# A fused conv/attention kernel: prologue in its own order, and q and k projected by three rounded products

## The chip, the cores and the metric

The kernel runs on one core of one Trainium2 chip. The metric is the device time of one execution in microseconds (us), as the median of the runs shown. Names of engines: PE is TensorE (matmul; PEld is its weight load), DVE is VectorE, ACT is ScalarE, POOL is GpSimd, SP is the sync engine that issues the DMAs.

## The reference, cut to what matters

The input is x of 16 images, 128 channels, 16 by 16 pixels, all float32. Four blocks follow each other.

```
L0: q = x as (b, 128, 256); energy = q q^T; attention = softmax(max - energy)
    out = attention q; se = sigmoid(w2 relu(w1 mean([x, out]))); x1 = se*x + (1-se)*out
L1: xr = relu(bn(depthwise3x3(reduce_w x1)))            # 64 channels
    2-D Fourier transform, 8-head attention on it, inverse transform; a gated filter
    x2 = post_w [out, filtered] + post_b + x1
L2: xn = group_norm(x2); q, k, v = w_qkv xn; 8-head attention over 256 pixels
    x3 = w_proj h + b_proj + x2
L3: q3, k3, v3 = conv3x3(x3); attention over the 16 images per pixel; layernorm; relu; conv3x3; + x3
```

## The kernel before, in words

**Tiling.** Images are handled in 8 pairs; channels lie on the 128 partitions and the two images of a pair side by side (512 columns). Each engine has one program written out by hand, and semaphores join them.

**Stages.** Blocks L0, L1 and the group norm are cut into small stages (function `stage(what, i)`, once per engine, for pair i): `energy`, `e_min`, `att0`, `att0t`, `o0`, `hid0`, `z0`, `se`, `x1` are L0; `red`, `taps0` to `taps2`, `xr`, `hid1`, `z1`, `xh`, `xht`, `dft`, `ab`, `squares`, `dot1`, `logit1`, `att1`, `even`, `filt`, `patt`, `post_att`, `y1`, `x2` are L1; `gsum`, `gvar`, `grstd`, `xn` are the group norm. `gvar` (L961) has four small DVE steps; `xn` (L970) has three small steps and two of 128x256.

**Slots.** `slots(j, late, early, cj)` is the body of a pair, 24 slots per engine: L2's attention of pair j, the L1 stages of pair j+1 (`late`), the L0 stages of pair j+2 (`early`) and the convolutions of L3 on the finished pair j-1 (`cj`). The tables `PE_SLOTS`, `ACT_SLOTS`, `DVE_SLOTS`, `POOL_SLOTS` (L65 to L71) say in which slot each stage stands. At the end of a body PE projects q and k of pair j+1 (`project`, L1345), ACT and DVE split them into a rounded and a low part (`qk_high_parts`, `qk_low_parts`), and the next body's scores need those. The convolutions and other products that must be exact are made of three products of operands rounded to fp32r (high*high, high*low, low*high). The projection uses one plain float32 product of 128x512 for each of its four blocks (L1358); the hardware runs each as two instructions.

**The prologue.** Before the first body, each engine walks its table for L0 of pair 0, then for L0 of pair 1 with L1 of pair 0 (L1084 to L1089 on DVE, L1587 to L1600 on PE). Before that DVE and PE wait for the first constants (`cst_loaded`, L857, L1575): DVE prepares seven small values, PE multiplies one bias. SP issues the loads in the order x_t (x by pixels, for the energies), x_in, first constants, second constants, weights. All stages of L1 take their matmul results from PSUM bank 1, each waiting until the stage before has read it. The program keeps PE occupied with idle products (`keep_busy`, L1249, matmuls of `ones_r`) in counts given by the `BUSY_` constants. For pairs 0 and 1 four of the nine depthwise taps are PE matmuls (`taps`, L1577); for the rest all nine are DVE operations (L900, L903).

## Time and profile before

| | |
|---|---|
| median of 3 runs | 492.95 us (491.77 to 495.27) |
| the profiled execution | 491.87 us, of which its span is 490.1 us |
| prologue, to the first score product of pair 0 | 44.1 us |
| bodies of pairs 0 and 1 | 44.1 to 134 us |
| bodies of pairs 2 to 6 | 134 to 359 us, 45.0 us each |
| body of pair 7, L3's attention, last convolutions | 359 to 490 us |

A row of the timeline gives the start, the length, the engine, the source line, the operation, what it writes from what, the shapes and a count; in brackets stands how long the engine had been idle and what ended that. A row of the chain of waits gives the start, the length and what ran: it is followed back from the last instruction, so that each piece was what the next one waited for. A row of stages gives for each stretch the busy time of each engine with the number of instructions, then TensorE's granted clock as a share of full speed and the DMA's load.

### The profile page before, as it was taken

Reading aid. Unit: us, or ns where it says so; the run is one execution under the profiler, and the core shown is the slowest. Engines: PE = TensorE matmul, PEld = TensorE weight load, DVE = VectorE, ACT = ScalarE, POOL = GpSimd, SP = SyncE. Lnnn points to the kernel's source line nnn. Section 1 sums busy time; section 2 is a strip of 40 time slices with the busy share of each in tenths; the row PEclk is TensorE's granted clock in tenths of the full one; section 3 lists DMA queues with packets and bytes.
Section 4 is the critical chain, followed back from the end, with each engine's and each line's share of the span. In section 5 each row is a group of like instructions: output and inputs, shape, how many; then the busy total and the mean of one; then the engine's idle time right before and its main releaser. Section 6 shows DMA issues by size and latency. Waiting matters only on the chain.

```text
span 490.1 us, 10552 instructions
## 1 busy us (share of the span) xinstructions
PE 462.6 (94%) x3790; PEld 371.5 (76%) x3790; DVE 342.4 (70%) x890; ACT 248.6 (51%) x590; POOL 125.3 (26%) x154
## 2 busy tenths in 40 slices
PE   8999999898999999999999999999997999998896
PEld 7876865676587778777776877777775789898895
DVE  1438567977787778688777877787476443776895
ACT  3434656665555555645656555545534531394551
POOL 5121363375012103101211121020110011332672
PEclk9999999999899999999999999999997999998998
DMA  7100012030002001000100000000000000005112
GB/s 274 36 32 3 1 49 91 1 93 24 0 1 60 7 0 43 21 0 0 43 21 0 0 21 0 2 22 3 0 1 23 1 23 1 1 1 171 45 56 73
DMA packets 10639, 15.28 MB, mean 31 GB/s; under 512 B 624, under 2 KB 8944, under 8 KB 10480
## 3 DMA queue, kind: packets, MB, share of 16 engines
q1 hardware_dynamic: 10608, 14.86, 9.4%
q8 instruction: 20, 0.33, 0.3%
q14 instruction: 11, 0.09, 0.1%
HBM read 10.66 MB, written 4.19 MB: 30 GB/s over the span
## 4 chain that ended last, share of the span: by engine, by line
PE 72%; DVE 13%; ACT 7%; issue 3%; POOL 3%; DMA 1%; SPq 0%; DVEq 0%; ACTq 0%; POOLq 0%
PE bank L1232 9%; PE bank L1234 8%; PE bank L1233 8%; PE bank L1358 5%; PE bank L1387 5%; PE bank L1450 5%; PE bank L1424 3%; PE bank L1252 3%; PE bank L1422 2%; PE bank L1478 2%; PE bank L1262 2%; ACT prob L751 2%; PE bank L1465 2%; PE bank L1274 2%; PE bank L1437 1%
## 5 line engine op out<-in xcount | busy, mean ns | idle before, releaser
L1232 PE MATMUL bank<-win,w_hi 128*128 128x256 f32 x360 | 108.4, 301 | 1.5 <-POOL win L592 1.2
L751 ACT ACTIVATE prob<-bank 128x512 f32<-128x512 f32 x128 | 69.6, 598 | 66.2 <-PE bank L1422 65.3
L1233 PE MATMUL bank<-win,w_hi 128*128 128x256 f32 x360 | 101.5, 282 | 0.0
L1234 PE MATMUL bank<-win,w_lo 128*128 128x256 f32 x360 | 101.5, 282 | 0.0
L1007 DVE TENSOR_REDUCE nmax<-bank 128x2 f32<-128x512 f32 x128 | 84.1, 685 | 15.0 <-PE bank L1387 14.5
L1232 PEld LDWEIGHTS bank<-win,w_hi 128*128 128x128 f32 x360 | 67.9, 189 | 7.2 <-POOL win L592 1.4
L1233 PEld LDWEIGHTS bank<-win,w_hi 128*128 128x128 f32 x360 | 68.1, 189 | 0.2
L1234 PEld LDWEIGHTS bank<-win,w_lo 128*128 128x128 f32 x360 | 68.0, 189 | 0.0
L540 POOL TENSOR_TENSOR first<-first 128x256 f32<-128x256 f32 x24 | 17.7, 738 | 149.7 <-ACT first L643 149.7
L1252 PE MATMUL bank<-ones_r 128*128 128x256 f32 x276 | 50.0, 319 | 1.1 <-DVE ones_r L856 1.1
L1252 PEld LDWEIGHTS bank<-ones_r 128*128 128x128 f32 x276 | 40.0, 209 | 5.5 <-issue 1.1
L1424 PE MATMUL bank<-qk 32*128 32x256 f32 x256 | 40.8, 336 | 2.0 <-DVE q_max L999 1.4
L1387 PE MATMUL bank<-qk 32*128 32x256 f32 x256 | 32.6, 332 | 8.9 <-ACT prob L751 6.6
L1450 PE MATMUL bank<-prob,v_t 128*32 128x256 f32 x512 | 35.1, 393 | 0.0
L1387 PEld LDWEIGHTS bank<-qk 32*128 32x128 f32 x256 | 19.5, 186 | 20.1 <-issue 8.4
L1424 PEld LDWEIGHTS bank<-qk 32*128 32x128 f32 x256 | 24.5, 188 | 12.4 <-issue 5.4
L1422 PE MATMUL bank<-q_max,qk 32*128 32x256 f32 x256 | 33.7, 281 | 0.0
L903 DVE SCALAR_TENSOR_TENSOR even<-red,cst,even 128x256 f32<-128x256 f32 x56 | 29.2, 522 | 2.4
L1358 PE MATMUL bank<-xn,cst 128*128 128x512 f32 x64 | 30.7, 605 | 0.0
L1422 PEld LDWEIGHTS bank<-q_max,qk 32*128 32x128 f32 x256 | 24.8, 191 | 0.0
L1450 PEld LDWEIGHTS bank<-prob,v_t 128*32 128x32 f32 x512 | 13.5, 110 | 14.8 <-issue 6.4
L999 DVE SCALAR_TENSOR_TENSOR q_max<-qk,cst,bank 128x512 fp32r<-128x512 f32 x16 | 11.9, 746 | 16.0 <-PE bank L1437 16.0
(246 smaller groups left out, 928.0 us busy)
## 6 DMA issues: line engine op xcount, KB each, us to landing
w_stage<-convs SPq DMA_DIRECT2D x4, 576.0 KB, 4.3
x_t<-x_px SPq DMA_DIRECT2D x8, 256.0 KB, 3.2
x_in<-x SPq DMA_DIRECT2D x8, 256.0 KB, 2.7
out<-x_pair SPq DMA_DIRECT2D x8, 256.0 KB, 2.2
q<-out SPq DMA_DIRECT2D x1, 2048.0 KB, 8.2
out<-v SPq DMA_DIRECT2D x8, 256.0 KB, 2.1
cst<-small SPq DMA_DIRECT2D x1, 1712.0 KB, 9.0
cst<-small SPq DMA_DIRECT2D x1, 253.5 KB, 3.7
```

Of the source, the lines that this page charges most:

```text
L751: act.activation(prob[:, x // 4 % 2, x % 4, :, :], bank[ST_BANK[x % 2]][:, :], ACT.Exp, scale=L2_SCALE).then_inc(st_exp, 1)
L903: dve.scalar_tensor_tensor(dwa, tap, wt, dwa, ALU.mult, ALU.add).then_inc(dw_tap, 1)
L1007: dve.tensor_reduce(nmax2[:, m, :, h // 4, col:col + 1], bank[s_bank(n)][:, :].rearrange("p (k s) -> p k s", k=CH), X, ALU.max, negate=Tru ...
L1232: mm(dst, hi, x_hi, start=(row == 0), stop=False)
L1233: mm(dst, hi, x_lo, start=False, stop=False)
L1234: return mm(dst, lo, x_hi, start=False, stop=(row == KH - 1))
L1252: mm(bank[unused][:, 0:HW], ones_r[:, :], ones_r[:, :].unsqueeze(1).to_broadcast([P, 2, P]), start=True, stop=True)
L1358: mm(dst, c("w" + what)[:, q * P:(q + 1) * P], xn_all, start=True, stop=True).then_inc(qk_done, 1)
L1387: ins = mm(bank[s_bank(x)][:, k * HW:(k + 1) * HW], q_hl[r, h // 4, m * HW + k * P:m * HW + (k + 1) * P], k_hi[r, h // 4, m * HW:(m + 1) * ...
L1422: ins = mm(dst, k_lo[r, h // 4, key], q_max[r, h // 4, :], start=False, stop=True)
L1424: mm(dst, k_hi[r, h // 4, key], q_hl[r, h // 4, m * HW:(m + 1) * HW], start=True, stop=False)
L1450: ins = mm(bank[O_BANK][a * SLOT:(a + 1) * SLOT, quad * HW:(quad + 1) * HW], v_t[:, m, k, 4 * quad + a, :], prob[:, g % 2, a, k, :], start ...
```

## The change

1. The prologue gets four tables of its own (`PE_FIRST`, `ACT_FIRST`, `DVE_FIRST`, `POOL_FIRST`). PE begins with the energies of pair 0 and waits for the constants after them, DVE prepares its values after `e_min`; L0 of pair 1 is begun before L1 of pair 0.
2. In the prologue the L1 stages of pair 0 use several PSUM banks (`chain_bank`), and waits that only guarded bank 1 are left out there; pair 1's x1 and its sum of taps lie in buffers of their own (`x3_pair`, `first`), so that its depthwise taps run on DVE between the steps of pair 0, and PE's taps of pair 1 behind `y1`.
3. q and k are projected by three products of rounded operands per block, all 128x512: high weights by high input, low weights by high input, high weights by low input. The split weights (`wqk_hi` on ACT, `wqk_lo` on DVE, 128x512 each) are made once in the prologue. For each pair ACT makes the high part of xn straight from x2 (two ACTIVATEs of 128x256, slot 20), DVE the low part (`xn_low`, one TENSOR_TENSOR of 128x512, slot 21). They lie in `win_1`, which is otherwise used only by pair 7.
4. The group norm's variance is one DVE step instead of two (`gvar`).
5. Several small tiles share memory (`ab_sq`, `logit1`, `att1`, `att1_n`, `post_att`, `h_t`).

```diff
@@ tables
+PE_FIRST = (("energy", 0, 2), ("bias", 0, 3), ("att0t", 0, 3), ("o0", 0, 8), ("hid0", 0, 2), ("z0", 0, 3),
...
+DVE_FIRST = (("e_min", 0), ("fixed", 0), ("att0_inv", 0), ("bias", 0), ("se", 0), ("x1", 0), ("e_min", 1), ("taps0", 0), ("taps1", 0), ("att0_inv", 1),
...
@@ names
+        xn_hi, xn_lo = [win_1[:, part, :, 0, 1:H + 1, :].rearrange("p a h t -> p a (h t)") for part in range(2)]
+        def chain_bank(what, i):
+
+            if is_pair(i, 0):
+                return bank[{"xht": 3, "dft": 4, "dot1": 3, "even": CONV, "filt": 4, "patt": 3}.get(what, 1)]
+            return bank[S2_BANK if what == "red" and is_pair(i, 1) else 1]
@@ ACT
+                if what == "xn":
+                    act.wait_ge(xn_done, 5 * i + 3)
+                    for m in range(2):
+                        act.activation(xn_hi[:, CH * m:CH * m + CH, :], x2[:, m, :].rearrange("p (k x) -> p k x", k=CH), ACT.Identity, bias=gb[:, m:m + 1],
+                                       scale=ga[:, m:m + 1]).then_inc(xn_high, 1)
...
+            for what, i in ACT_FIRST:
...
+                if what == "wqk":
+                    act.wait_ge(cst2_loaded, 16)
+                    act.activation(wqk_hi[:, :], wqk, ACT.Copy).then_inc(wqk_high, 1)
@@ DVE
-                    dve.tensor_tensor(gm2[:, :], gmv[:, :, 1], gm2[:, :], ALU.subtract).then_inc(gn_chain, 1)
-                    dve.wait_ge(gn_chain, 7 * i + 7)
-                    dve.tensor_scalar(gvar[:, :], gm2[:, :], 1e-5, None, ALU.add).then_inc(gvar_done, 1)
+                    dve.scalar_tensor_tensor(gvar[:, :], gmv[:, :, 1], 1e-5, gm2[:, :], ALU.add,
+                                             ALU.subtract).then_inc(gvar_done, 1)
...
+                if what == "xn_low":
+                    dve.wait_ge(xn_done, 5 * i + 5)
+                    dve.wait_ge(xn_high, 2 * i + 2)
+                    dve.tensor_tensor(xn_lo, xn[:, :, :].rearrange("p m (k x) -> p (m k) x", k=CH), xn_hi.bitcast(F32),
+                                      ALU.subtract).then_inc(xn_low, 1)
@@ PE
                 if what == "even":
-                    pe.wait_ge(logit1_done, i + 1)
+                    if not is_pair(i, 0):
+                        pe.wait_ge(logit1_done, i + 1)
...
                 if what == "q":
-                    pe.wait_ge(xn_done, 5 * i + 5)
+                    if isinstance(i, int) and i == 0:
+                        pe.wait_ge(wqk_low, 1)
+                    pe.wait_ge(xn_high, 2 * i + 2)
...
-                        mm(dst, c("w" + what)[:, q * P:(q + 1) * P], xn_all, start=True, stop=True).then_inc(qk_done, 1)
+                        mm(dst[q], wqk_hi[:, cols], x_hi, start=True, stop=False)
+                        mm(dst[q], wqk_lo[:, cols], x_hi, start=False, stop=False)
+                        if what == "k":
+                            mm(dst[q], wqk_hi[:, cols], x_lo, start=False, stop=True).then_inc(qk_done, 1)
+                    if what == "q":
+                        pe.wait_ge(xn_low, i + 1)
+                        for q in quads:
+                            mm(dst[q], wqk_hi[:, q * P:(q + 1) * P], x_lo, start=False, stop=True).then_inc(qk_done, 1)
...
-            pe.wait_ge(cst_loaded, 16)
-            mm(bank[CONV][:, 0:1], c("wproj"), c("bv"), start=True, stop=True).then_inc(bias_mm, 1)
...
+            for what, i, busy in PE_FIRST:
+                if what == "taps":
+                    taps(i)
+                if what == "bias":
+                    pe.wait_ge(cst_loaded, 16)
+                    mm(bank[CONV][:, 0:1], c("wproj"), c("bv"), start=True, stop=True).then_inc(bias_mm, 1)
+                stage(what, i)
+                keep_busy(busy)
```

The start of PE's program, before. `ones_r` is an idle product, `bank<-cst` the bias, `x_t` the energies, `cst,att` the transposes of stage `att0t`:

```order
L1252 MATMUL bank<-ones_r 128x256 x14
L1576 MATMUL bank<-cst 128x1
L1262 MATMUL bank<-x_t 128x128 x4
L1252 MATMUL bank<-ones_r 128x256 x9
L1268 MATMUL bank<-cst,att 128x128 x2
```

And now:

```order
L1300 MATMUL bank<-ones_r 128x256 x13
L1310 MATMUL bank<-x_t 128x128 x4
L1300 MATMUL bank<-ones_r 128x256 x2
L1657 MATMUL bank<-cst 128x1
L1300 MATMUL bank<-ones_r 128x256 x3
L1316 MATMUL bank<-cst,att 128x128 x2
```

The energies now stand ahead of the product that waits for the constants.

The end of the prologue on PE, before, from the group sums (`stats`) over pair 1's `red` and its taps (`red,q`) to the projection (`xn,cst`) and the first scores (`qk`):

```order
L1342 MATMUL bank<-stats,cst 128x4
L1343 MATMUL bank<-stats,cst 128x4
L1252 MATMUL bank<-ones_r 128x256 x3
L1288 MATMUL bank<-x,cst 64x256 x2
L1252 MATMUL bank<-ones_r 128x256 x4
L1583 MATMUL bank<-red,q 128x256 x4
L1358 MATMUL bank<-xn,cst 128x512 x4
L1387 MATMUL bank<-qk 128x256 x4
```

And now:

```order
L1648 MATMUL bank<-red,q 128x256 x4
L1300 MATMUL bank<-ones_r 128x256 x2
L1398 MATMUL bank<-stats,cst 128x4
L1399 MATMUL bank<-stats,cst 128x4
L1300 MATMUL bank<-ones_r 128x256 x22
L1418 MATMUL bank<-win,wqk_hi 128x512
L1419 MATMUL bank<-win,wqk_lo 128x512
L1418 MATMUL bank<-win,wqk_hi 128x512
L1419 MATMUL bank<-win,wqk_lo 128x512
L1425 MATMUL bank<-win,wqk_hi 128x512 x2
```

Pair 1's `red` and taps have moved ahead of the group sums, and the projection's first products wait for nothing of pair 1's taps.

DVE in the body of pair 0, from pair 1's normalised input (`xn`) to its first taps for pair 2 (`even<-red`), now:

```order
L1019 TENSOR_SCALAR xn<-x,ga,gb 128x256
L1069 TENSOR_TENSOR x_pair<-bank,x_res 128x256 [waits x2_res_done,proj_done]
L941 TENSOR_SCALAR even<-red,cst 128x256 [waits red_copied]
L944 SCALAR_TENSOR_TENSOR even<-red,cst,even 128x256 [waits dw_tap] x2
L1024 TENSOR_TENSOR win<-xn,win 128x4x128 [waits xn_high,xn_done]
L944 SCALAR_TENSOR_TENSOR even<-red,cst,even 128x256 [waits dw_tap,red_copied]
```

The row `win<-xn,win` is `xn_low`; it is new, and stands between the third and the fourth of nine taps.

## Rows read from the trace of the kernel before

**Rows 1.** The page's busy time of TensorE

```profile
PE 462.6 (94%) x3790; PEld 371.5 (76%) x3790; DVE 342.4 (70%) x890; ACT 248.6 (51%) x590; POOL 125.3 (26%) x154
```

**Rows 2.** Busy time by stage

```profile
88.00:134.00 46.00, 41.98 (x347) 31.52 (x348) 36.95 (x85) 26.43 (x62) 20.30 (x21) 0.96 0.11 31
...
179.00:224.00 45.00, 44.14 (x378) 33.74 (x377) 35.08 (x93) 24.91 (x61) 7.42 (x10) 1.00 0.06 17
...
122.00:124.00 2.00, 2.00 (x10) 1.50 (x11) 1.65 (x7) 0.53 (x2) 0.71 (x1) 0.50 0.00 0
```

**Rows 3.** Waits of PE from 134 to 360 us

```profile
PE bank L1387 <- ACT prob L751: 3.4, 5, 0.7
```

**Rows 4.** Chain of waits: prologue, then the turn from pair 0 to 1

```profile
0.75 0.41 SPq L433
...
1.68 3.68 DMA cst<-small
5.41 0.59 PE bank L1576 x2
...
38.77 1.93 PE bank L1583 x8
40.70 3.43 PE bank L1358 x8
44.14 0.50 PE bank L1387 x4
...
86.00 1.32 DVE qk L987 x2
```

**Rows 5.** Timeline of the prologue, instructions at which its segments meet

```profile
1.06 3.35 PE L1252 MATMUL bank<-ones_r 128*128 128x256 f32 x14 [1.06 <-DVE ones_r L856]
...
5.86 2.06 PE L1262 MATMUL bank<-x_t 128*128 128x128 f32 x8
...
19.68 0.60 ACT L681 ACTIVATE xr<-even,bn_shift,bn_scale 128x256 f32<-128x256 f32 x1 [3.12 <-DVE even L908]
...
23.09 0.38 PE L1303 MATMUL bank<-cst,xh_ab 128*128 128x128 f32 x2
...
25.91 0.38 ACT L695 ACTIVATE xh_ab<-bank 128x256 f32<-128x256 f32 x1
...
29.61 0.39 ACT L701 ACTIVATE att<-logit,nmax 128x128 f32<-128x128 f32 x1
...
34.47 0.87 DVE L949 SCALAR_TENSOR_TENSOR x<-bank,cst,x 128x256 f32<-128x256 f32 x2 [0.98 <-PE bank L1338]
...
41.65 1.58 ACT L723 ACTIVATE qk<-bank,bq_lo,cst 128x512 fp32r<-128x512 f32 x2 [3.02 <-PE bank L1358]
```

**Rows 6.** The tile x_t: landing of its three loads before 30 us

```profile
DMA to landing us min/median/max: 2.9/3.3/5.2
```

**Rows 7.** Timeline: three rounded products of a convolution, in a row

```profile
139.87 0.28 PE L1232 MATMUL bank<-win,w_hi 128*128 128x256 f32 x1
139.99 0.28 PE L1233 MATMUL bank<-win,w_hi 128*128 128x256 f32 x1
140.11 0.28 PE L1234 MATMUL bank<-win,w_lo 128*128 128x256 f32 x1
```

**Rows 8.** Lines L1036 (DVE) and L698 (ACT): ns min/median/max

```profile
L1036 DVE TENSOR_TENSOR win<-windows,win x16: 673/692/1076, 106.6 to 401.4; 128x512 fp32r<-128x512 f32 x16
...
L698 ACT ACTIVATE even<-bank x8: 384/400/418, 29.3 to 332.8; 128x256 f32<-128x256 f32 x8
```

**Rows 9.** Timeline: turn from pair 3 to 4, and from pair 0 to 1

```profile
217.58 0.35 DVE L900 TENSOR_SCALAR even<-red,cst 128x256 f32<-128x256 f32 x1
...
222.44 1.40 DVE L987 SCALAR_TENSOR_TENSOR qk<-bank,cst,qk 128x512 fp32r<-128x512 f32 x2
...
220.04 1.88 PE L1358 MATMUL bank<-xn,cst 128*128 128x512 f32 x4
...
225.20 0.50 PE L1387 MATMUL bank<-qk 32*128 32x256 f32 x4
...
81.73 4.26 DVE L903 SCALAR_TENSOR_TENSOR even<-red,cst,even 128x256 f32<-128x256 f32 x8
```

More of the change, by code:

```diff
@@ L236, in program @@
         o2 = sb("o2", [P, QUADS, HW])
-        h_t = sb("h_t", [P, CH, C])
+        h_t = xh_t
         x2_res = sb("x2_res", [P, 2, HW])
@@ L558, in _ @@
             pool.memset(win_1[:, :, :, :, :, :].bitcast(F32), 0.0).then_inc(pool_set, 1)
-            for s in range(SLOTS):
-                for what, i in parts(POOL_SLOTS, s, 0, None):
-                    stage(what, i)
-            for s in range(SLOTS):
-                for what, i in parts(POOL_SLOTS, s, 1, 0):
-                    stage(what, i)
+            for what, i in POOL_FIRST:
+                stage(what, i)
             pool.wait_ge(vec_set, 6)
@@ L1082, in slots @@
                 normalise(j, 1)
-            for s in range(SLOTS):
-                for what, i in parts(DVE_SLOTS, s, 0, None):
-                    stage(what, i)
-            for s in range(SLOTS):
-                for what, i in parts(DVE_SLOTS, s, 1, 0):
-                    stage(what, i)
+            for what, i in DVE_FIRST:
+                if what == "fixed":
+                    fixed()
+                if what == "bias":
+                    bias()
+                stage(what, i)
+                if what == "wqk":
+                    dve.wait_ge(wqk_high, 1)
+                    dve.tensor_tensor(wqk_lo[:, :], wqk, wqk_hi[:, :].bitcast(F32), ALU.subtract).then_inc(wqk_low, 1)
             dve.wait_ge(pool_set, 7)
@@ L1331, in stage @@
-                    mm(bank[1][:, 0:C], att1_n[:, :], c("post1"), start=True, stop=True).then_inc(patt_done, 1)
+                    if not is_pair(i, 0):
+                        pe.wait_ge(filt_scaled, i + 1)
+                    mm(chain_bank(what, i)[:, 0:C], att1_n[:, :], c("post1"), start=True, stop=True).then_inc(patt_done, 1)
                 if what == "y1":
                     pe.wait_ge(patt_copied, i + 1)
+                    if is_pair(i, 0):
+                        pe.wait_ge(even_copied, 1)
+                        pe.wait_ge(filt_scaled, 1)
@@ L1353, in project @@
                 if what in "qk":
+                    w_at = "qk".index(what) * QUADS * P
+                    dst = [bank[b][:, :] for b in (FRONT if what == "q" else ST_BANK)]
                     for q in quads:
```

190 lines of the change are left out of this document (99 added, 91 removed).

## The prediction, made before the changed kernel ran

> **What bounds the kernel now.** I read the page's busy shares first: TensorE is busy for 94% of the span, DVE for 70%, ACT for 51% [rows 1]. That average hides stages with different limits, so the table by stage comes next. In the body of a middle pair (45.0 us long) PE is busy for 44.14 us, DVE for 35.08, ACT for 24.91 [rows 2]. The list of PE's waits there agrees: over five bodies, 134 to 360 us, its largest entry is 3.4 us in five waits for ACT's exponentials, 0.7 us each [rows 3]. In these bodies a microsecond less of PE work on its own queue is a microsecond less of time, if nothing else falls behind. From 88 to 134 us PE is busy for 41.98 of 46.0 us only [rows 2]; there the chain of waits runs through DVE, POOL and loads. So it does in the prologue, where the chain begins with SP's issues at 0.75 us, the load of the first constants (1.68 to 5.36 us) and the bias product that waits for them, and ends with pair 1's PE taps (38.77), the projection (40.70) and the first scores at 44.14 us [rows 4]. The change touches three places: the prologue, the turn from the body of pair 0 to that of pair 1, and the six later turns where pairs 2 to 7 are projected.
>
> **The prologue.** I add it up in segments between instructions that the timeline shows [rows 5], each against what now stands in the queues.
>
> Start of the energies: 5.86 us before, behind the bias product. Now x_t is waited for alone: issued at 0.75 [rows 4], it lands after 2.9, 3.3 or 5.2 us [rows 6], and the 13 idle products that are left of 14 (3.35 us from 1.06 [rows 5]) end at 4.2. I take 3.3, the median, so 4.1 us and -1.8; the ends are 3.7 us (-2.2) and 6.0 us (nothing). DVE's seven small values, now behind `e_min`, and POOL's memsets behind them still end ahead of the first `diff0`.
>
> The same shift holds to `xr` (19.68) as long as pair 1's energies, which now stand ahead of pair 0's `red`, have their x_t. Before, they stood behind all of this, and the load was hidden completely; that cover is gone. The load is queued behind the second constants and the weights; landing up to 5.2 us after an issue at 6 to 8 us is 11 to 13 us, and `red` wants to start at 13.6. Eight instructions of energies take 1.0 us warm and 2.06 as at 5.86. I charge +0.3, with ends 0 and +1.2.
>
> From `xr` to the transposes `xht` (L1303): 3.4 us before, because energies and idle products of pair 1 lay between. Now PE has `hid0` of pair 1 in front, which waits for two ACT steps behind the gate's. By ACT's steps it is again 3.4 us. Nothing.
>
> From there to the copy of the transform (L695): 2.8 us before, with ACT and PE taken by pair 1's attention. Now the copy out of PSUM, eight 128x128 instructions and the hand-over: 2.1 us, -0.7.
>
> From there to the exponential `att1` (L701): 3.7 us before. Now pair 1's `red` is copied by ACT ahead of it and PE has two more float32 products first: 3.8 us, +0.1.
>
> To `x2` (L949): 4.9 us before, by way of the filter, which no longer stands in between. Now DVE sets the end: the exponential and the reciprocal 0.7, `att1_n` 0.5, a tap 0.5, `post_att` 0.4, two taps 1.0, the low weights 0.7 (a 128x512 subtraction [rows 8]): 3.8 us, -1.1.
>
> To ACT's first q part (L723): 7.2 us before, the last part of it spent on pair 1's taps on PE, which are now done earlier. Now one small DVE step less (-0.2), two ACTIVATEs of about 0.4 [rows 8] instead of waiting, then five rounded products ahead of the first finished block: 7.1 us, -0.1. To the first scores 2.5 us before, 2.4 now, as DVE has no tap sum in front.
>
> Sum: -1.8 + 0.3 - 0.7 + 0.1 - 1.1 - 0.1 - 0.1 = -3.4; I take -3.2, because hand-overs that a sum on paper misses only ever add. Ends: -1.5 (late loads, half of the middle segments) and -4.2.
>
> **The turn from pair 0 to pair 1.** The chain of waits runs through DVE here: eight taps from 81.73 and then the two low parts of q, which the chain has at 86.00 [rows 4, 9]. `xn_low` stands between these taps: 0.69 us by the same kind of subtraction with the same strided operand, at most 1.08 beside POOL [rows 8]. PE's shorter projection helps nothing, as it waits for DVE. +0.7; ends 0 (if the wait for POOL or a load ends later anyway) and +1.0. In the body of pair 1 everything behind it moves along.
>
> **The later turns.** A float32 block costs two instructions; eight of them take 3.43 us in the chain [rows 4], 0.43 each, so four blocks of a pair 3.44 us. A rounded product is one instruction; with 256 columns they start 0.12 us apart [rows 7]. No row shows one with 512 columns. If all of the 0.12 scales, it is 0.24; if it is 256 columns at 2.4 GHz (0.107) and a fixed 0.012, it is 0.225. Ends: 0.213 and 0.24. Twelve take 2.7 us at 0.225 (2.56 to 2.88), so a pair gains 0.74 us (0.56 to 0.88). Six turns where PE is the bound: -4.4, from -3.4 to -5.3.
>
> What could eat it: ACT's two new steps (0.8 us) stand two slots and a product of values ahead of PE's projection; ACT is idle for 20 of 45 us [rows 2], so they hide. DVE gains 0.69 us of work between its taps and gives back 0.2. In the turn from pair 3 to 4 DVE's taps begin at 217.58, its q parts run from 222.44 to 223.84, and PE's scores start at 225.20 [rows 9]. With `xn_low` the first q part is ready at 223.8 and the second at 224.5, while PE would now be there at 225.20 - 0.74 = 224.46. The first scores need only the first part. So the new work just fits; another 0.7 us would not. I charge nothing.
>
> TensorE's column rate deserves a look at the notes. The rows show 0.12 us for 256 columns. The Trainium skill, page "TensorE: Matmul & The Clock Gate", section "Back-to-back issue gap", gives for streams of weight load and matmul about 131 ns per 512-column matmul, against 216 ns for an isolated one. By 0.131 the twelve would take 1.57 us and the six turns would gain 11.2 us instead of 4.4. The rows speak against it, since half the columns already cost nearly as much.
>
> **Sum.** -3.2 + 0.7 - 4.4 = -6.9 us. Against the profiled execution (491.87 us, span 490.1) that is 485.0; it lies 1.08 us below the median of the runs, and two of the three runs are 491.77 and 492.95. I set out from between these, 492.4: 485.5 us.
>
> **Rivals.**
> First, DVE becomes the bound at each turn. For it: the fit above has no slack behind the first q part, and row maxima queue behind it. Against: the kernel before left 1.36 us between DVE's last q part and PE's scores. If the six gains vanish, -3.2 + 0.7 is left: 489.9 us.
> Second, the early order doesn't pay in full: pair 1's x_t comes late, or PE, with fewer idle products in the prologue, drops to 1.2 GHz there. The trace has such a drop, at 122 to 124 us the granted clock is 0.50, which is the lower of its two levels, in a stage in which PE was idle for 4 of 46 us [rows 2]. Half of the prologue's gain lost: 487.1 us.
> Third, on the other side: a 512-column rounded product costs what a float32 instruction of that size costs, 0.43 us. Then twelve take 5.16 us instead of 3.44, +1.72 a turn, +10.3 over six, and about +1.2 in the prologue: 492.4 - 2.5 + 10.3 + 1.2 = 501.4 us. It decides for slower from 0.32 us a product (12 x 0.32 = 3.44 + 2.5/6). Against it: 256 columns at 0.12 us, strided like the new operand.
> Fourth, the rule of 0.131 us: 492.4 - 2.5 - 11.2 = 478.7 us, as each product would stream at nearly twice the rate of [rows 7].
>
> **How the numbers follow.** The forecast has 0.78, the first rival 0.11, the second 0.06, the third 0.03, the fourth 0.02. The forecast's own range is 482.6 to 488.5 (the ends of the three terms don't fall together; the clock's drop of 122 us, worth some 1.5 us, may go or come twice). Taking in the second rival and part of the first: 482.2 to 489.4. One per cent, 4.9 us, is about what a measurement of this kernel tells from no change, so faster means below 488.0. Most of the forecast, most of the second rival and the fourth lie there: 0.79. The rest of these and the first: 0.18. Slower: 0.03.
>
> **What would show it.** In the changed profile the first score product stands at 41 us; the energies start near 4.1, `x2` of pair 0 near 31. Twelve projection products of a pair take 2.7 us, and a middle body 44.3 us. `xn_low` takes 0.69 us. I am wrong if these products start more than 0.25 us apart, if PE waits for DVE's q parts at the turns, if the first scores stand behind 43 us, or if the granted clock falls before them.

## The result, and the profile after

The changed kernel takes 486.85 us in the median of twelve executions, against 492.94 us for the kernel before beside it; the ratio is 0.9883, with a 95% interval of 0.9858 to 0.9907. (One of the twelve executions took 1398 us; this one, and single executions over 1.5% above the fastest of their kernel, one each in e_prologue_only, e_gvar_only and e_xt_ahead_again, are left out of the ratios but not of the medians.) Two later comparisons of the same kernel gave 0.9902 (0.9863 to 0.994) and 0.9895 (0.9872 to 0.9917). The forecast was 485.5 us, with a range from 482.2 to 489.4. The profiled execution took 486.65 us, its span is 484.9 us: 5.2 less than before. (Counted from first scores to first scores, a middle body of the kernel before took 44.87 us and the body of pair 6 41.96; the 45.0 us of the table ahead are a mean over rounded borders, 134 to 359 where the scores have 135.3 to 356.9.)

The page's first part, busy time by engine, answers to [rows 1]:

```profile
PE 453.7 (94%) x3792; PEld 373.6 (77%) x3792; DVE 346.3 (71%) x891; ACT 254.5 (52%) x607; POOL 125.0 (26%) x154
```

TensorE lost 8.9 us of busy time and keeps its share. DVE and ACT, which now make the low and high parts of xn, are busy for 3.9 and 5.9 us more, and the span still fell.

The table by stage, with the two stages of [rows 2] and the one that replaces its third line (columns as there; the third number from the end is the granted clock):

```profile
88.00:134.00 46.00, 42.45 (x359) 33.18 (x356) 36.98 (x87) 28.71 (x67) 20.36 (x21) 0.96 0.11 32
179.00:224.00 45.00, 44.12 (x389) 35.13 (x388) 36.26 (x95) 25.58 (x63) 7.41 (x10) 1.00 0.06 17
...
90.00:96.00 6.00, 5.93 (x33) 5.15 (x34) 5.05 (x13) 4.44 (x11) 2.42 (x3) 0.72 0.01 3
```

In 45 us of the middle TensorE is as busy as before, but a body now takes 44.27 us where it took 44.87, so the stretch holds more of the next one. DVE is up by 1.2 us there. The list of PE's waits from 126 to 356 us answers to [rows 3]:

```profile
PE bank L1454 <- ACT prob L782: 3.4, 5, 0.7
PE bank L1491 <- DVE q_max L1044: 0.4, 1, 0.4
PE bank L1545 <- ACT h_c L747: 0.2, 1, 0.2
```

It is the same entry of 3.4 us in five waits, and nothing on it names DVE's low parts of q. The later turns are still bound by TensorE. The timeline of the turn from pair 3 to 4, first PE and then DVE, answers to [rows 9]:

```profile
216.31 0.40 PE L1418 MATMUL bank<-win,wqk_hi 128*128 128x512 f32 x1
216.55 0.39 PE L1419 MATMUL bank<-win,wqk_lo 128*128 128x512 f32 x1
216.78 0.40 PE L1418 MATMUL bank<-win,wqk_hi 128*128 128x512 f32 x1
217.02 0.40 PE L1419 MATMUL bank<-win,wqk_lo 128*128 128x512 f32 x1
217.25 0.63 PE L1425 MATMUL bank<-win,wqk_hi 128*128 128x512 f32 x2
...
220.85 0.50 PE L1454 MATMUL bank<-qk 32*128 32x256 f32 x4
...
215.16 0.69 DVE L1024 TENSOR_TENSOR win<-xn,win 128x512 fp32r<-128x512 f32 x1
215.76 3.57 DVE L944 SCALAR_TENSOR_TENSOR even<-red,cst,even 128x256 f32<-128x256 f32 x6
219.25 1.41 DVE L1032 SCALAR_TENSOR_TENSOR qk<-bank,cst,qk 128x512 fp32r<-128x512 f32 x2
```

The starts of the products are 0.235 us apart. From the first of them to the scores it is 4.54 us, where [rows 9] have 5.16 (220.04 to 225.20): a turn gained 0.62 us. DVE ends its q parts at 220.66, just ahead of the scores.

The prologue, from the timeline: the instructions of [rows 5] that changed most, and the first scores.

```profile
4.00 1.87 PE L1310 MATMUL bank<-x_t 128*128 128x128 f32 x8
...
7.35 0.15 DVE L893 TENSOR_SCALAR bn_tmp<-cst 128x1 f32<-128x1 f32 x1 [1.01 <-DMA cst<-small]
...
13.96 1.13 PE L1310 MATMUL bank<-x_t 128*128 128x128 f32 x8
...
41.92 0.50 PE L1454 MATMUL bank<-qk 32*128 32x256 f32 x4 [0.57 <-ACT qk L758]
```

The energies of pair 0 start at 4.00, as forecast. But the first constants were used at 5.39 us before, and here at 7.35 (they landed at 5.37 and 7.32), and the chain of waits begins with them all the same:

```profile
1.68 5.64 DMA cst<-small
7.32 0.04 issue
7.37 0.38 PE bank L1657 x2
7.75 0.47 PE bank L1300 x3
8.21 0.23 PE bank L1316 x2
```

TensorE sits behind the bias product (L1657) until the constants come, and the transposes of `att0` (L1316) stand behind that. The first scores are at 41.92, 2.2 us earlier than in [rows 4]; with the constants on time the repeat (e_after_again) has them at 41.14.

By pair 7 the scores stand 6.2 us earlier (356.91 and 350.73), yet the spans differ by 5.2 only: what follows took 133.2 us before and 134.2 now. Over the fourteen profiles of this study this last part takes 132.9 to 134.6 us, 134.1 in that of e_gvar_only, whose kernel is nearly the one before, so the 1.0 us can't be laid to the change.

### The profile page after: what moved, and what is told of

It is laid out like the page before. It is cut to its first block, busy times and chain, and to the rows that moved or that the text cites. A ratio compares the mean times of both kernels' runs of the same rounds, so it can differ in the third digit from the quotient of the medians.

```text
span 484.9 us, 10582 instructions
## 1 busy us (share of the span) xinstructions
PE 453.7 (94%) x3792; PEld 373.6 (77%) x3792; DVE 346.3 (71%) x891; ACT 254.5 (52%) x607; POOL 125.0 (26%) x154
## 4 chain that ended last, share of the span: by engine, by line
PE 70%; DVE 13%; ACT 8%; issue 4%; POOL 3%; DMA 2%; SPq 0%; DVEq 0%; ACTq 0%; POOLq 0%
PE bank L1280 9%; PE bank L1281 8%; PE bank L1282 8%; PE bank L1454 5%; PE bank L1517 5%; PE bank L1491 3%; PE bank L1300 3%; PE bank L1489 2%; PE bank L1545 2%; ACT prob L782 2%; PE bank L1532 2%; PE bank L1418 2%; PE bank L1310 2%; PE bank L1322 1%; PE bank L1504 1%
## 5 line engine op out<-in xcount | busy, mean ns | idle before, releaser
L1300 PE MATMUL bank<-ones_r 128*128 128x256 f32 x246 | 44.9, 316 | 1.1 <-DVE ones_r L888 1.1
L1300 PEld LDWEIGHTS bank<-ones_r 128*128 128x128 f32 x246 | 35.0, 203 | 5.0 <-DVE ones_r L888 1.1
L944 DVE SCALAR_TENSOR_TENSOR even<-red,cst,even 128x256 f32<-128x256 f32 x52 | 27.5, 528 | 1.8
L1044 DVE SCALAR_TENSOR_TENSOR q_max<-qk,cst,bank 128x512 fp32r<-128x512 f32 x16 | 11.9, 747 | 16.0 <-PE bank L1504 15.9
L669 ACT ACTIVATE first<-bank 128x512 f32<-128x512 f32 x24 | 14.3, 597 | 16.6 <-PE bank L1282 16.6
## 6 DMA issues: line engine op xcount, KB each, us to landing
cst<-small SPq DMA_DIRECT2D x1, 253.5 KB, 5.6
```

Of the source, the lines that this page charges most:

```text
L944: dve.scalar_tensor_tensor(dwa, tap, wt, dwa, ALU.mult, ALU.add).then_inc(dw_tap, 1)
L1300: mm(bank[unused][:, 0:HW], ones_r[:, :], ones_r[:, :].unsqueeze(1).to_broadcast([P, 2, P]), start=True, stop=True)
```

## The experiments

All times in this table are from profiles. "Constants" is the first use of the first constants on DVE (in the new order `e_min` stands ahead of it, so it can come later than their landing), "pair 1" the start of its energies, a body runs from a pair's first scores to the next pair's, the middle body is the mean over pairs 3 to 5. A star marks a body in which the granted clock fell to 0.5, for 3.4 us or, in e_constants_ahead and e_gvar_only, for 6.8; e_projection_only has two such falls in body 1. Pair 1's energies stood behind other work in the old order and are not listed there.

| kernel | constants | pair 1 | first scores | body 0 | body 1 | middle | span |
|---|---|---|---|---|---|---|---|
| before | 5.39 | – | 44.14 | 42.70 | 48.48* | 44.87 | 490.1 |
| changed | 7.35 | 13.96 | 41.92 | 43.00 | 47.41* | 44.27 | 484.9 |
| e_after_again | 5.91 | 13.28 | 41.14 | 44.37* | 47.96* | 44.25 | 485.3 |
| e_after_third | 7.21 | 14.96 | 42.93 | 44.29* | 46.47 | 44.24 | 486.2 |
| e_prologue_only | 6.03 | 13.36 | 40.49 | 44.01* | 47.90* | 44.87 | 487.8 |
| e_projection_only | 6.69 | – | 45.74 | 42.99 | 48.61* | 44.24 | 489.6 |
| e_gvar_only | 5.38 | – | 44.38 | 42.83 | 50.05* | 44.89 | 492.9 |
| e_xt_ahead | 7.04 | 12.42 | 41.86 | 43.13 | 47.99* | 44.27 | 486.0 |
| e_xt_ahead_again | 6.30 | 12.08 | 39.93 | 44.40* | 46.47 | 44.24 | 483.2 |
| e_constants_ahead | 5.35 | 13.43 | 41.24 | 44.08* | 49.53* | 44.26 | 487.3 |
| e_low_twice | 6.11 | 13.43 | 41.70 | 44.99* | 48.16* | 44.31 | 486.3 |
| e_more_idle | 5.52 | 13.51 | 42.50 | 44.73 | 47.06 | 44.25 | 486.6 |
| e_xt_idle_1 | 6.29 | 11.99 | 39.96 | 43.11 | 48.61* | 44.21 | 483.2 |
| e_four_products | 5.70 | 13.69 | 42.99 | 44.03 | 48.56* | 45.16 | 494.3 |

**The parts by themselves.** e_prologue_only keeps the new prologue and projects q and k with float32 products as before:

```diff
-                        mm(dst[q], wqk_hi[:, cols], x_hi, start=True, stop=False)
-                        mm(dst[q], wqk_lo[:, cols], x_hi, start=False, stop=False)
...
+                        mm(dst, c("w" + what)[:, q * P:(q + 1) * P], xn_all, start=True, stop=True).then_inc(qk_done, 1)
```

> The changed kernel's prologue and variance step, but q and k projected by four plain float32 products as before, without xn's high and low parts and the split weights. Theory (three separate terms): only the prologue's gain is left, 2.2 us as the two profiles stand at the first scores plus some 0.7 us of split weights on DVE that fall away, so 490 us against 493; the turn from pair 0 to 1 costs nothing, middle bodies take 45.0 us. Rival (the prologue's gain comes from the shorter projection): 493 us.

Measured: 489.93 us, ratio 0.9946 (0.9915 to 0.9977). The first scores come at 40.49 and the middle body keeps its 44.87 us. The prologue pays by itself, and it pays there alone. Its scores are 0.65 us ahead of the repeat's 41.14, with pair 1's energies at the same place (13.36 and 13.28): by these two profiles the new projection, with its split weights, costs that much of the prologue's gain. The new banks, buffers and orders of the prologue were run only together.

e_projection_only has the order of the prologue as before and the new projection in every pair, with the variance in one step.

```diff
-            for what, i, busy in PE_FIRST:
+            for s in range(SLOTS):
+                for what, i in parts(PE_SLOTS, s, 0, None):
```

> The old prologue order, with rounded products for q and k and the one-step variance (the split weights are made between pair 0's and pair 1's stages). Theory: six later turns give 0.62 us each by the pace of 0.235 us a product, the turn from pair 0 to 1 takes back 0.4, so 3.3 us less than before, 489.5 us; middle bodies 44.3 us. Rival (DVE or a later wait eats it): 493 us.

Measured: 490.79 us, ratio 0.9944 (0.9914 to 0.9974). The middle body is at 44.24 us, so the whole gain of the later turns is the projection's. The two halves add up: 0.54% and 0.56% less, against 1.17% and, in the repeats, 0.98% and 1.05% for both. Its own prologue is worse than before (first scores at 45.74): the constants came at 6.69, the granted clock was at 0.5 from 7.3 to 10.8 us, and the weights have to be split in an order that has no room made for it. How much each did was not taken apart.

e_gvar_only puts the variance into one step in the kernel before:

```diff
-                    dve.tensor_tensor(gm2[:, :], gmv[:, :, 1], gm2[:, :], ALU.subtract).then_inc(gn_chain, 1)
-                    dve.wait_ge(gn_chain, 7 * i + 7)
-                    dve.tensor_scalar(gvar[:, :], gm2[:, :], 1e-5, None, ALU.add).then_inc(gvar_done, 1)
+                    dve.scalar_tensor_tensor(gvar[:, :], gmv[:, :, 1], 1e-5, gm2[:, :], ALU.add,
+                                             ALU.subtract).then_inc(gvar_done, 1)
```

> The kernel before with the variance in one DVE step instead of two. Theory: 0.2 us in the prologue, nothing in the bodies where DVE is not the bound: 492.7 us, no difference that can be measured. Rival (the group norm's chain ends every body): 8 x 0.2 = 1.6 us less.

Measured: 492.71 us, ratio 0.9977 (0.9948 to 1.0006): no difference that can be told, and the middle body stays at 44.89 us. Item 4 of the change is worth nothing measurable.

**The changed kernel again**, with no edit, twice:

> The changed kernel once more, unchanged, to see which details of its profile repeat: the first constants landing at 7.35 us instead of 5.38, TensorE's granted clock at half between 9 and 12.5 us, and the clock's drops in the bodies of pairs 1 and 7. If the late constants come from the new order, they are there again (first scores at 41.9 us); if it was a stray of one load, the first scores stand at 41 us. Time 486.5 us.

Measured: 488.51 us, ratio 0.9902 (0.9863 to 0.994).

> The changed kernel once more, unchanged, as the measure for the three that run beside it on the same chip. Both theories expect a ratio to the kernel before of 0.988 to 0.990, and a load of pair 1's x_t that lands at 13.3 to 13.5 us, or constants behind 7 us and then energies near 14.

Measured: 487.27 us, ratio 0.9895 (0.9872 to 0.9917). Both have the middle body at 44.24 to 44.25 us. Their prologues differ by 1.8 us. In the first, the constants had landed at 5.33, and what TensorE then waited for, in its timeline, was a transfer:

```profile
4.01 1.52 PE L1310 MATMUL bank<-x_t 128*128 128x128 f32 x8
...
13.28 1.16 PE L1310 MATMUL bank<-x_t 128*128 128x128 f32 x8 [1.55 <-DMA x_t<-x_px]
...
18.67 0.60 ACT L707 ACTIVATE xr<-even,bn_shift,bn_scale 128x256 f32<-128x256 f32 x1 [0.38 <-DVE even L949]
```

The chain of waits has the same load:

```profile
5.56 7.67 DMA x_t<-x_px
13.23 0.04 issue
13.28 1.16 PE bank L1310 x8
```

When this load was issued hardly mattered. In the eleven profiles in which it stands behind the second constants and the first weights it was issued at 5.2 to 6.8 us in the new order and at 7.9 to 8.7 us in the old, and it landed at 13.2 to 13.7 us in all of them, each time 0.60 to 0.66 us behind the weights.

In the third run of the changed kernel TensorE waited for the constants instead (landed at 7.19), and its products ran at the lower pace until 14 us:

```profile
4.00 2.00 PE L1310 MATMUL bank<-x_t 128*128 128x128 f32 x8
...
7.23 0.59 PE L1657 MATMUL bank<-cst 128*128 128x1 f32 x2 [0.81 <-DMA cst<-small]
...
11.08 2.27 PE L1300 MATMUL bank<-ones_r 128*128 128x256 f32 x8
...
14.96 1.13 PE L1310 MATMUL bank<-x_t 128*128 128x128 f32 x8
```

Eight idle products take 2.27 us here and 1.30 us in the other repeat. Their starts, 256 columns each, are 0.213 us apart until 13 us, as in the stretch of the first profile for which the record of the granted clock has 0.50 (9.1 to 12.5 us): that is 1.2 GHz, the lower of the two levels. The table by stage prints 1.00 here, but the trace has no record of the clock ahead of 14.0 us in this profile. Here the late constants come with both a wait and the lower pace behind it.

**Pair 1's x_t ahead of the weights.** The wait of 1.55 us above is the risk for which the prediction had charged 0.3 us. e_xt_ahead moves one load:

```diff
+            load_x_t(1)
             load_weights(0)
-            load_x(1)
+            load_x_in(1)
             load_x(2)
```

> The changed kernel with one line of SP's program moved: the 512 KB load of pair 1's x_t is issued ahead of the first weights' load, everything else as it was. In the repeat of the changed kernel the energies of pair 1 waited 1.55 us for that load and ran at 13.28, and xr ended its wait at 18.67; the prediction had priced this wait at 0.3. Theory A (that wait is on the prologue's path): the energies of pair 1 run near 11.9 without a wait on a transfer, xr starts 0.7 to 1.2 us earlier, the first scores come near 40.3 (41.14 in the repeat), and the median is 0.7 us less than the changed kernel's 486.85: 486.1. Theory B (the chain of pair 0 on VectorE and ScalarE ends last anyway): the wait goes and the first scores stay within 0.2 us of 41.14, the time within noise of 486.85.

(The load has 256 KB by the list of DMA issues, not the 512 KB of this text.) Measured: 485.3 us, ratio 0.9849 (0.9812 to 0.9885). The wait is gone and pair 1's energies stand at 12.42, but in the profiled execution the constants were late (landed at 7.02) and the clock was at 0.5 from 20.7 to 24.1 us, so its first scores say little. Hence once more:

> The changed kernel with pair 1's x_t loaded ahead of the first weights, once more: its profile had the energies of pair 1 at 12.42 without a wait on the transfer, but constants that landed at 7.04 and a granted clock of 0.5 from 21 to 24 us, so its first scores (41.86) tell little. Theory A (the wait was on the path): first scores near 40.3 in a profile without that fall of the clock, and a median 0.7 to 1.5 us under that of the third run of the changed kernel beside it. Theory B (the gain seen in the median, 485.3, was the chip's): within 0.4 us of it.

Measured: 485.37 us, ratio 0.9852 (0.9822 to 0.9881), beside 487.27 us for the changed kernel on the same chip: 1.9 us less, though the two intervals of the ratios overlap a little, and this median is of four executions (485.01, 484.86, 485.73 and 492.75). Its timeline:

```profile
3.97 1.06 PE L1317 MATMUL bank<-x_t 128*128 128x128 f32 x8
...
12.08 1.16 PE L1317 MATMUL bank<-x_t 128*128 128x128 f32 x8 [0.29 <-DMA x_t<-x_px]
...
17.47 0.60 ACT L714 ACTIVATE xr<-even,bn_shift,bn_scale 128x256 f32<-128x256 f32 x1 [0.38 <-DVE even L956]
...
39.93 0.50 PE L1461 MATMUL bank<-qk 32*128 32x256 f32 x4 [0.58 <-ACT qk L765]
```

All three stand 1.2 us ahead of the repeat with constants on time (13.28, 18.67, 41.14). The load was on the prologue's path with 1.2 us. What the medians show beyond that, 0.7 us, has no place in this profile. This version has the lowest ratio of the study, twice. The load now lands at 11.9 to 12.0 us, 0.60 to 0.64 us behind the second constants, and in this profile pair 1's energies start as soon as it has (12.04 and 12.08); issuing it ahead of these too was not run.

**What the early energies are worth.** e_constants_ahead keeps the new order but for the start:

```diff
-PE_FIRST = (("energy", 0, 2), ("bias", 0, 3), ("att0t", 0, 3), ...
+PE_FIRST = (("bias", 0, 0), ("energy", 0, 5), ("att0t", 0, 3), ...
-DVE_FIRST = (("e_min", 0), ("fixed", 0), ("att0_inv", 0), ("bias", 0), ...
+DVE_FIRST = (("fixed", 0), ("bias", 0), ("e_min", 0), ("att0_inv", 0), ...
```

> The changed kernel with the bias product back ahead of the energies on TensorE, and the constants' small operations and the bias back ahead of the row minimum on VectorE; the number of idle products between them is the same. Theory A (the early energies are worth what the forecast gave them, 1.8 us, and the order of the rest pays apart from them): the energies of pair 0 start near 5.9 again, the first scores come 1.4 to 1.9 us later than the repeat's 41.14, near 42.8, and the median is near 488.5. Theory B (the prologue is bound later by the transfer of pair 1's x_t or by the work of pair 1, so the start is worth little): first scores within 0.6 us of 41.14 and a median under 487.5.

Measured: 487.95 us, ratio 0.9924 (0.9896 to 0.9953). The profile takes theory B's side, the median (B wanted less than 487.5, A about 488.5) neither's. Pair 0's energies start at 5.61 instead of 4.01, and the wait of pair 1's energies for x_t shrinks to match:

```profile
5.61 1.14 PE L1310 MATMUL bank<-x_t 128*128 128x128 f32 x8
...
13.43 1.16 PE L1310 MATMUL bank<-x_t 128*128 128x128 f32 x8 [0.49 <-DMA x_t<-x_px]
```

The first scores are at 41.24, 0.1 us behind the repeat's. The load was issued at 6.78 us here and at 5.56 there, and landed at 13.39 and 13.23. So with the constants on time, and while the load lands near 13.3 us, the early start is worth 0.1 us in the profile and not 1.8. The median lies some 1.5 us above the changed kernel's by its ratio, more than this profile shows; with a fall of the clock of 6.8 us in its body 1 (from 120.8 us), one profile can't say whether that is the start's worth in other executions. That stays open.

**VectorE at the turns.** e_low_twice does the new subtraction twice:

```diff
+                    for n in range(2):
+                        if n:
+                            dve.wait_ge(xn_low, 2 * i + 1)
                         dve.tensor_tensor(xn_lo, ...
```

> The changed kernel with VectorE's subtraction that makes xn_low (128x512, 0.69 us) done twice in every pair, the second after a wait for the first. The prediction held that VectorE just fits at the turns and that another 0.7 us would not. Theory A (the prediction's): each of the seven turns pays 0.4 to 0.7 us, the turn from pair 2 on included; the middle bodies are 44.7 to 44.9 us long instead of 44.26, and the median is 3 to 5 us more than 486.85: 490 to 492. Theory B (at the later turns VectorE's low parts of q have room behind them, since the scores start 0.9 us after them): turn 0 to 1 pays 0.7 us, the middle bodies stay at 44.26 to 44.35, and the median is 0.5 to 1.5 us more: 487.3 to 488.4.

Measured: 489.79 us, ratio 0.9949 (0.9922 to 0.9975). The profile takes theory B's side: from pair 0's first product to pair 1's scores it is now 6.28 us (80.41 to 86.69) where the changed kernel has 5.55 (79.37 to 84.92), 0.73 more, while the middle body grows from 44.27 to 44.31 us only. In DVE's timeline at the turn from pair 3 to 4 the extra step is absorbed:

```profile
217.76 1.41 DVE L1027 TENSOR_TENSOR win<-xn,win 128x512 fp32r<-128x512 f32 x2
219.09 3.44 DVE L944 SCALAR_TENSOR_TENSOR even<-red,cst,even 128x256 f32<-128x256 f32 x6
222.45 1.40 DVE L1035 SCALAR_TENSOR_TENSOR qk<-bank,cst,qk 128x512 fp32r<-128x512 f32 x2
```

The last q part ends at 223.85, and the scores stand at 223.53: only the first part is waited for, and it is ready at 223.15.

At the turn from pair 0 to 1 TensorE's timeline shows where the step goes. First the kernel before:

```profile
81.58 1.98 PE L1358 MATMUL bank<-xn,cst 128*128 128x512 f32 x4
...
86.84 0.50 PE L1387 MATMUL bank<-qk 32*128 32x256 f32 x4
```

Then the changed one, with its DVE step:

```profile
80.46 0.68 DVE L1024 TENSOR_TENSOR win<-xn,win 128x512 fp32r<-128x512 f32 x1
...
81.20 0.73 PE L1425 MATMUL bank<-win,wqk_hi 128*128 128x512 f32 x2 [0.63 <-DVE win L1024]
...
84.92 0.50 PE L1454 MATMUL bank<-qk 32*128 32x256 f32 x4
```

And with the step doubled:

```profile
82.96 0.73 PE L1428 MATMUL bank<-win,wqk_hi 128*128 128x512 f32 x2 [1.35 <-DVE win L1027]
```

L1425 holds the third products of q (high weights by low xn). They wait for `xn_low`, which stands behind three taps on DVE: 0.62 or 0.63 us in all ten profiles that have the step once, 1.35 with it twice, 0.72 more, and that is the 0.73 of this turn. At the later turns no such wait is in any trace.

The median is higher than these two terms make it (about 2.7 us over the changed kernel by the ratios, 1.0 by the terms), and what the rest is was not found. Five of its twelve executions had a mean granted clock of 0.973 or less, against two of the changed kernel's eleven, so a part may be falls of the clock.

**The clock's falls.** Each profile has some (in the bodies of pairs 0 and 1 all but one), and e_more_idle tries to fill TensorE's waits in the first two bodies:

```diff
-BUSY_AHEAD, BUSY_EVEN, BUSY_PAIR_1 = 13, 2, {s: 3 for s in range(13)}
-BUSY_PAIR_0 = {1: 6, 2: 6, 3: 6, 4: 6, **{s: 3 for s in range(5, 16)}, 16: 6, 17: 6, 18: 6, 19: 6}
+BUSY_AHEAD, BUSY_EVEN, BUSY_PAIR_1 = 13, 2, {s: 5 for s in range(13)}
+BUSY_PAIR_0 = {1: 6, 2: 6, 3: 6, 4: 6, **{s: 5 for s in range(5, 16)}, 16: 8, 17: 8, 18: 8, 19: 8}
```

> The changed kernel with more idle products in the bodies of pairs 0 and 1: five instead of three in the slots that had three, eight instead of six in the last four of pair 0. Theory A (the stretches of 4 us at a granted clock of 0.5 to 0.7 that every profile shows somewhere between 72 and 126 us are due to idle stretches on TensorE, and each costs about 1.3 us): no such stretch is left before 130 us, the body of pair 1 ends 1 to 1.5 us sooner relative to its start, and the median is 1 to 1.5 us less: 485.5. Theory B (the drops come whatever TensorE does there, or the idle products push work back as much as the clock gives): the granted clock still falls between 70 and 130 us, or it doesn't and the two bodies are no shorter; the median is 486.5 to 488.

Measured: 488.87 us, ratio 0.9951 (0.9926 to 0.9976). The granted clock stays at 1.00 through both bodies (it fell before them, from 14 to 18 us, behind a wait of 2.17 us for pair 1's x_t) (the table by stage):

```profile
42.50:87.20 44.70, 43.85 (x377) 34.20 (x377) 30.46 (x68) 27.11 (x64) 18.35 (x19) 1.00 0.13 39
87.20:134.30 47.10, 45.17 (x392) 35.78 (x391) 38.45 (x88) 29.57 (x69) 20.55 (x21) 1.00 0.11 31
```

But body 0 takes 44.73 us, more than with a fall (44.08 to 44.40) and 1.7 more than without, and body 1 takes 47.06, 0.6 more than the 46.47 that the changed kernel has there when the clock holds. That the added products push the work back is the likely reason. The profile is theory B's, and the median lies above both theories, about 2.9 us over the changed kernel by the ratios. I tried them in pair 1 alone, on top of the early load:

> The load of pair 1's x_t ahead, and five idle products instead of three in each of the first 13 slots of pair 1's body, pair 0's left as it is. With more idle products in both, pair 0's body came to 44.73 us (43.0 in the changed kernel's first profile), pair 1's to 47.06 (47.41 and 47.96 in the changed kernel's two, each with a fall of the clock). Theory A (in pair 1 the idle products fill waits, in pair 0 they pushed work back): the clock doesn't fall between 86 and 130 us, the body of pair 1 from its first scores to the next takes 46.9 to 47.1, and the median is 0.5 us under e_xt_ahead_again's. Theory B (they cost what they save): the body takes 47.4 or more, and the median is the same or above.

```diff
-BUSY_AHEAD, BUSY_EVEN, BUSY_PAIR_1 = 13, 2, {s: 3 for s in range(13)}
+BUSY_AHEAD, BUSY_EVEN, BUSY_PAIR_1 = 13, 2, {s: 5 for s in range(13)}
```

Measured: 486.34 us, ratio 0.9883 (0.9858 to 0.9908): nothing gained over e_xt_ahead_again. The clock fell in pair 1 in spite of them, and the body took 48.61 us:

```profile
118.00:122.00 4.00, 4.00 (x23) 2.93 (x21) 3.59 (x14) 1.47 (x3) 0.71 (x1) 0.57 0.00 0
```

**The price of a product.** e_four_products adds the product of the low weights with the low xn to each quarter of q and k (a part of the sum that the changed kernel leaves away):

```diff
+                            mm(dst[q], wqk_lo[:, cols], x_lo, start=False, stop=False)
                             mm(dst[q], wqk_hi[:, cols], x_lo, start=False, stop=True).then_inc(qk_done, 1)
```

> The changed kernel with a fourth product for each quarter of q and k (low weights by low xn), four more products of 512 columns in each pair, two each for q and k. Theory A (a product costs 0.235 us of TensorE's time at the turns, nothing hides it and nothing else sets the turn): the middle bodies are 44.26 + 0.94 = 45.2 us long if each pair has four more, and with two quarters each for q and k that is four; six middle turns give 5.6 us, the prologue and the turn 0 to 1 about 1.5 together, and the median is 7 us more than the changed kernel's, 493 to 494. Theory B (VectorE's and ScalarE's parts set the turn as well, so TensorE's time shows only in part): middle bodies of 44.3 to 44.9, and 488 to 491 in all.

Measured: 496.05 us, ratio 1.0074 (1.0048 to 1.01). PE's timeline at the turn from pair 2 to 3:

```profile
175.44 0.40 PE L1418 MATMUL bank<-win,wqk_hi 128*128 128x512 f32 x1
175.68 0.40 PE L1419 MATMUL bank<-win,wqk_lo 128*128 128x512 f32 x1
175.91 0.40 PE L1418 MATMUL bank<-win,wqk_hi 128*128 128x512 f32 x1
176.14 0.40 PE L1419 MATMUL bank<-win,wqk_lo 128*128 128x512 f32 x1
176.38 0.39 PE L1426 MATMUL bank<-win,wqk_lo 128*128 128x512 f32 x1
176.61 0.39 PE L1427 MATMUL bank<-win,wqk_hi 128*128 128x512 f32 x1
```

The pace is 0.235 us again, the middle body 45.16 us: four products add 0.9 us, nearly the 0.94 that the pace makes. Theory A holds for the bodies. In all it cost 2 us more than theory A's 493 to 494: in its profile the first scores are 1.85 us later than the repeat's, with a fall of the clock from 14.8 to 18.2 us, and there is another at 332.2 to 335.7 us, a place where no other profile has one.

## Why the prediction was right

**The later turns (-0.74 each, -4.4).** The mechanism held in every run: TensorE is the bound, and a product fewer is time gained. The size of the term was a little off. The products start 0.235 us apart, so the upper of the two scalings of [rows 7] was the right one (0.12 for 256 columns, twice that for 512), and I had taken 0.225 for a part that doesn't scale. Twelve take 2.82 us; a turn gained 0.62 (5.16 to 4.54; the middle body 0.60). Six turns give -3.7 by that. In the two profiles the scores of pair 7 stand 6.2 us earlier (356.91 and 350.73): 2.2 from the prologue, -0.3 from body 0, and 4.3 from bodies 1 to 6, in which body 1, with a fall of the clock in both, has 1.1.

**Fit of DVE there (nothing charged).** Right, and with more room than I saw. "Another 0.7 would not" fit was wrong: e_low_twice put it there and a middle body grew by 0.04 us. The sum had the first q part some 0.6 us ahead of the scores (223.8 and 224.46), so by its own figures another 0.7 would have cost hardly 0.1. It is ready 0.9 us ahead of them now (219.25 + 0.70 against 220.85), since TensorE gained 0.12 us less than I took and the new step lengthened DVE's stretch from its first tap to its q parts by 0.54 us (4.86 to 5.40) and not by 0.69. The second subtraction lengthened it by 0.6 more, so that 0.38 were left.

**The turn from pair 0 to 1 (+0.7).** It cost 0.3: body 0, in profiles without a fall of the clock in it, went from 42.70 and 42.83 us to 42.99, 43.00, 43.11 and 43.13. The step was wrong here. The forecast let `xn_low` delay DVE's q parts and took TensorE's shorter projection for worth nothing, "as it waits for DVE". The traces show TensorE working without a break from the projection's first product (81.58) to the scores (86.84) in the kernel before, so its own work was the bound; and now it waits 0.63 us for `xn_low` itself, at L1425. By the pace of 0.235 us that product would start at 80.40 and it starts at 81.20, 0.8 us late; the shorter projection gives back 0.62; from the first product to the scores it is 5.55 us (79.37 to 84.92) against 5.26. The rest, 0.1 us, is the first product, after which the next starts 0.34 us later. Ahead of the first product body 0 is unchanged (37.44 us from the first scores in both profiles). The measured 0.3 lies in the forecast's range, and that is luck: two effects that it didn't have cancel in part. With `xn_low` ahead of the taps in this body the wait should shrink; that was not run.

**The prologue (-3.2).** With the constants on time the first scores are at 41.14 (-3.0), with late constants at 41.92 and 42.93 (-2.2 and -1.2); the forecast had 41. The energies start 1.86 us earlier, as forecast, but `xr` moved by 1.0 only (19.68 to 18.67 in the repeat), where the two terms together had -1.5. Pair 1's load (+0.3, ends 0 and +1.2) costs 1.2, its upper end: with it issued earlier `xr` stands at 17.47. The mistake is in how the load was timed. The forecast took 5.2 us from issue to landing [rows 6] and added them to the new issue; but that 5.2 was this same load, issued at 7.94 and landing at 13.18 behind the constants and the weights. Issued at 5.56 it took 7.67. While it lands there, the start is not what sets `xr`, as e_constants_ahead shows with 0.1 us for it. The 2.2 us that `xr` gains without that wait are not the start's alone either: TensorE's pace differs, with idle products 0.213 us apart until 9.4 us in the profile before and 0.118 from 5.9 us in the repeat, and the eight energies took 2.06 and 1.52 us. Whether the new order brought the earlier rise of the clock was not tested.

Behind `xr` the segments came out nearly one by one. Repeat against forecast: 3.2 (3.4) to `xht`, 2.1 (2.1) to the copy of the transform, 3.8 (3.8) to `att1`, 3.6 (3.8) to `x2`, 7.6 (7.1) to the first q part, 2.2 (2.4) to the first scores; together 22.5 where the forecast had 22.6 and the kernel before 24.5. The one miss has a cause in part: the two ACTIVATEs of xn's high part, taken at 0.4 us each from a row of another line, took 1.09 together (0.59 each).

**Late constants** were not among the terms. The forecast let the bias product stand behind the energies at no cost; when the constants land at 7.2 or 7.3 instead of 5.4 us, TensorE stops there, and the price is that of the second rival (half of the prologue's gain lost), by another cause than its two. The new order did not make them late by itself: one of the three profiles with the old order has them late too (landed at 6.66, e_projection_only), and the load is issued at 1.68 us in every profile. By the list of what would show the steps wrong, the clock was not to fall ahead of the first scores; in the first profile it did, from 9.1 to 12.5 us.

**The rivals.** The first (DVE at each turn, 489.9 us) is refuted by the list of waits and, in the profile, by e_low_twice. The third (0.43 us a product) and the fourth are both refuted by the pace of 0.235 us. For the fourth, the Trainium skill, page "TensorE: Matmul & The Clock Gate", section "Back-to-back issue gap", has about 131 ns for a 512-column matmul in a stream; here it is 0.235 us in every profile that has such products, and the measurement decides.

**The sum.** Terms as measured: -3.0 (prologue with constants on time) + 0.3 - 3.7 = -6.4 us, and -5.6 with the constants as in the first profile, against 6.1 us between the medians. The forecast's -6.9 was too large by 0.7 for the six turns and 0.2 for the prologue, and too small by 0.4 for the turn from pair 0 to 1: the total is closer than its terms.

## What to carry to other kernels

Before crediting an instruction that starts sooner, look up when the next transfer on its path lands: a start 1.6 us earlier bought 0.1 us in the profile, and issuing one load of 256 KB ahead of a larger one that nobody needed yet bought 1.2. A load's time from issue to landing, read in one place, doesn't move with the issue when other loads stand ahead of it. When a new step feeds products as well as lengthens a queue, follow both consumers: here the wait was for the step itself, and not behind it. To learn whether an engine has slack at a hand-over, double its new step: the same 0.7 us cost 0.73 at one turn and 0.04 at the others, in the profile. Where a price scales by columns and the trace has no row of the right size, take plain proportion before you invent a fixed part.

## What the runs showed of the hardware that was not expected

- The load of the first constants (253.5 KB, issued at 1.68 us in every profile) landed at 5.0 to 5.5 us in nine of the fourteen profiles, and at 6.28, 6.66, 7.02, 7.19 and 7.32 in the others. In the three in which that was later than 7 us TensorE waited for it. Two of these had the lower pace afterwards: eight idle products take 2.27 us instead of 1.30 (e_after_third, until 14.0 us), or the granted clock is at 0.5 from 9.1 to 12.5 (changed); in the third (e_xt_ahead) it fell only at 20.7. The two longest waits for pair 1's x_t, 2.17 and 2.18 us, had a fall 0.8 and 1.1 us behind them, the three of 1.5 us had none. So a late load can cost pace beside its wait; no run isolates it.
- Pair 1's x_t (256 KB) landed 0.60 to 0.66 us behind the load issued before it, whether it was issued at 5.2 or at 8.7 us.
- TensorE starts at its lower level in every profile: idle products of 256 columns start 0.213 us apart from 1.4 to 4 us. The record of the clock begins at 3.9 to 14.0 us, and where there is no record the table by stage prints 1.00; the pace of a known product tells the level.
- A fall of the granted clock to 0.5 in the body of pair 0 or 1 is a part of nearly every execution profiled, and its place changes between executions of the same kernel: in body 0 and body 1, in body 0 alone, or in body 1 alone for the changed kernel. A body 0 with one is longer by 1.0 to 1.4 us (44.08 to 44.40 against 42.99 to 43.13), a body 1 by 0.9 to 1.5 for a fall of 3.4 us (47.41 to 47.99 in the changed kernel and e_xt_ahead, against 46.47). No run sets the fall apart from the idle time that goes with it. TensorE had idled ahead of each: it was busy for 2.49 of the 4 us ahead of the fall at 122 us in the kernel before. The same idle stretch (from 116.5 us) has no fall behind it in e_after_third. More idle products left no fall in the bodies of one kernel (e_more_idle) and one in those of another (e_xt_idle_1).
- A rounded product of 512 columns by 128x128 weights starts every 0.235 us, one of 256 columns every 0.118, each with a weight load of its own: twice the columns, twice the time.
